# TensorE's order in a macaron block: a group's values and the output projection's halves move behind V's projection

## The reference, cut to what matters

```
x = x + 0.5 * stack(layernorm(x))       # 6 layers of attention + feed-forward
x = x + mamba(layernorm(x))             # gated convolution and a selective scan over 16 states
x = x + 0.5 * stack(layernorm(x))       # the same 6 layers again
```

```
q, k, v = split(shift(x) @ Wqkv[i])                  # 16 heads of 64
q, k = rotary(l2norm(q) * qs), rotary(l2norm(k) * ks)
sim  = q @ k' * 8, masked, windows of 32 queries against the 64 keys of this and the window before
x    = x + (softmax(sim) @ v) @ Wo[i]
h    = layernorm(shift(x)) * g + b
a, gate = split(h @ W1[i] + b1)
x    = x + (a * gelu(gate)) @ W2[i] + b2
```

## Time and profile before

| | us |
|---|---|
| median of 3 runs | 3372.07 (3358.28 to 3372.07) |
| profiled execution | 3364.97 |
| its span, first to last instruction | 3363.2 |
| PE busy | 2891.1 (86%) |
| DVE busy | 2933.3 (87%) |
| POOL busy | 2423.5 (72%) |
| ACT busy | 2059.8 (61%) |
| mean granted clock, share of full speed | 0.946 |

### The profile page before, as it was taken

How to read it: one execution, slowest core, us unless ns; L and a number is a source line. 1 busy time by engine, 2 the same in 40 slices (tenths; PEclk the granted TensorE clock), 3 DMA queues, 4 the chain that set the end, 5 groups by cost and what they waited for, 6 DMA issues and landing times. The chain is left out here.

```text
span 3363.2 us, 132089 instructions
## 1 busy us (share of the span) xinstructions
PE 2891.1 (86%) x57914; PEld 1829.9 (54%) x57914; DVE 2933.3 (87%) x4224; ACT 2059.8 (61%) x3820; POOL 2423.5 (72%) x1679
## 2 busy tenths in 40 slices
PE   5689988988999989897677788999998989998987
PEld 3455555655666655553233455555565555555553
DVE  6789989999999988986898789889899989898984
ACT  3466666666676666665663566666566666566663
POOL 3678787787787787874464678778787787787773
PEclk8899999999999999998897899999999999999998
DMA  5233333333333333320002233333343333342330
GB/s 136 65 80 77 82 91 74 84 92 71 84 92 73 89 85 72 88 65 28 10 4 59 68 81 78 75 93 77 73 101 73 86 90 71 82 94 65 88 74 15
DMA packets 114726, 250.85 MB, mean 75 GB/s; under 512 B 27244, under 2 KB 60648, under 8 KB 114152
## 3 DMA queue, kind: packets, MB, share of 16 engines
q1 hardware_dynamic: 114152, 242.40, 30.5%
HBM read 37.82 MB, written 3.15 MB: 12 GB/s over the span
## 5 line engine op out<-in xcount | busy, mean ns | idle before, releaser
L1096 ACT ACTIVATE squares<-general 128x512 f32<-128x512 f32 x768 | 453.7, 597 | 716.8 <-PE general L661 707.8
L1290 POOL TENSOR_TENSOR probs<-probs,row_sum 128x1024 f32<-128x1024 f32 x192 | 365.4, 1903 | 442.4 <-DVE row_sum L968 442.3
L1270 POOL TENSOR_TENSOR q_ring<-q_ring,partner 128x512 f32<-128x512 f32 x384 | 491.0, 1279 | 203.9 <-DMA partner<-sines 203.3
L881 DVE TENSOR_TENSOR sines<-general,layer_tables 128x512 f32<-128x512 f32 x768 | 515.8, 672 | 85.3 <-ACT squares L1096 81.8
L1270 POOL TENSOR_TENSOR k_ring<-k_ring,partner 128x512 f32<-128x512 f32 x384 | 490.9, 1278 | 0.0
L695 PE MATMUL general<-probs_t,v_buf 32*64 32x64 f32 x24576 | 339.0, 234 | 153.8 <-issue 85.1
L659 PE MATMUL general<-xs_hi,wqkv_lo 128*128 128x512 f32 x768 | 454.2, 591 | 18.5 <-DVE xs_lo L908 8.0
L695 PEld LDWEIGHTS general<-probs_t,v_buf 32*64 32x64 f32 x24576 | 304.0, 134 | 246.1 <-issue 237.5
L1284 POOL TENSOR_TENSOR probs<-probs,q_scale 128x1024 f32<-128x1024 f32 x192 | 365.4, 1903 | 15.1
L722 PE MATMUL general<-k_ring,q_ring 64*32 64x64 f32 (+1 forms) x24576 | 295.3, 223 | 92.5 <-issue 53.1
L671 PE MATMUL general<-att,wo 128*128 128x512 f32 x768 | 366.2, 621 | 4.6 <-ACT att L1166 4.2
(11 more groups left out here) (233 smaller groups left out, 6369.9 us busy)
## 6 DMA issues: line engine op xcount, KB each, us to landing
partner<-sines SPq DMA_DIRECT2D x1536, 128.0 KB, 2.3
wqkv_raw<-in_wqkv SPq DMA_DIRECT2D x80, 208.0 KB, 2.7
wo<-in_wo SPq DMA_DIRECT2D x12, 512.0 KB, 5.1
w<-in_w SPq DMA_DIRECT2D x12, 341.0 KB, 3.2
base_dram<-x SPq DMA_DIRECT2D x8, 256.0 KB, 2.4
att<-in_wqkv SPq DMA_DIRECT2D x2, 1024.0 KB, 6.7
sines<-base_dram SPq DMA_DIRECT2D x8, 256.0 KB, 3.9
w<-in_w SPq DMA_DIRECT2D x12, 128.0 KB
```

Of the source, the lines that this page charges most:

```text
L881: e.tensor_tensor(by_seq(sines[:, i % 2, which, :]), g, both(layer_tables[:, 2 * which + 1, :]), ALU.mult).then_inc(S[f"sin_{side}"], 1)
L1096: e.activation(squares[:, (2 * p + which) % 4, :], general_of(("proj", k, n, p, which))[:, :], ACT.Square).then_inc(S[f"squared_{side}"], 1)
L1270: e.tensor_tensor(y, y, partner[:, i % 2, which, :], ALU.add).then_inc(S[f"rotated_{side}"], 1)
L1290: e.tensor_tensor(y, y, spread_keys(row_sum[:, i % 2, :]), ALU.mult).then_inc(S["probs_done"], 1)
```

## The change

In `tensor_stack` V's projection now follows K's directly, then come the halves of the output projection (the second asked for before the first; they never share a substep), and the group's values last. The first half of the output projection had stood behind Q's projection and before the scores and the gates. `Banks.stack` walks in the same new order, so the banks and the waits on them change too.

```
@@ Banks.stack
-            if st.out_first:
-                n, i = st.out_first
-                self.use(("project", k, n, i), "att_added", (g + n) * 2 + i + 1)
...
+            if st.v:
+                n, p = st.v
+                self.use(("v", k, n, p), "v_kept", (g + n) * PAIRS + p + 1)
+            if st.out_last is not None:
+                self.use(("project", k, st.out_last, 1), "att_added", (g + st.out_last) * 2 + 2)
+            if st.out_first is not None:
+                self.use(("project", k, st.out_first, 0), "att_added", (g + st.out_first) * 2 + 1)
             if st.values:
                 n, group = st.values
                 for j in range(4):
                     self.use(("att", k, n, group, j), "att_kept", ((g + n) * GROUPS + group) * 4 + j + 1)
-            if st.out_last is not None:
-                self.use(("project", k, st.out_last, 1), "att_added", (g + st.out_last) * 2 + 2)
-            if st.v:
-                n, p = st.v
-                self.use(("v", k, n, p), "v_kept", (g + n) * PAIRS + p + 1)
@@ tensor_stack
                 if st.spread:
                     pe_spread(e, w, k, *st.spread)
-                if st.out_first:
-                    pe_out(e, w, k, *st.out_first)
                 if st.scores:
...
                 if st.now:
                     pe_project(e, w, k, *st.now, 1)
+                if st.v:
+                    pe_v(e, w, k, *st.v)
+                if st.out_last is not None:
+                    pe_out(e, w, k, st.out_last, 1)
+                if st.out_first is not None:
+                    pe_out(e, w, k, st.out_first, 0)
                 if st.values:
                     pe_values(e, w, k, *st.values, range(0, NWIN // 2))
-                if st.out_last is not None:
-                    pe_out(e, w, k, st.out_last, 1)
                 if st.values_rest:
                     pe_values(e, w, k, *st.values_rest, range(NWIN // 2, NWIN))
-                if st.v:
-                    pe_v(e, w, k, *st.v)
```

More of the change, by code:

```diff
@@ L34 @@
 POOL_BANKS = 7
[L37 to L45, removed]
+SCORES_LAG = 10
+SCORES_REST_LAG = 10
+SCALE_LAG = 10
+OFF_LAG = 11
+EXP_LAG = 12
+PROBS_LAG = 12
+TURN_LAG = 13
+VALUES_LAG = 14
+VALUES_REST_LAG = 14
+KEPT_LAG = 14
 V_LAG = 1
-SPREAD_LAG = SCORES_LAG
+SPREAD_LAG = 10
 PROBS = 2
@@ L108, in __init__ @@
         self.exps = self.group(t, EXP_LAG)
+        self.probs = self.group(t, PROBS_LAG)
         self.turn = self.group(t, TURN_LAG)
@@ L120, in __init__ @@
         self.spread = self.group(t, SPREAD_LAG)
-        self.out_first = next(((self.item(t, at), i) for i, at in ((0, 17),) if self.item(t, at) is not None), None)
+        self.out_first = self.item(t, 17)
+        self.first_added = self.item(t, 17)
         self.out_last = self.item(t, 21)
+        self.last_added = self.item(t, 21)
+        self.shift = self.item(t, 21)
         self.center = self.item(t, 22)
         self.var = self.item(t, 23)
+        self.var_turn = self.item(t, 23)
         self.root = self.item(t, 24)
         self.gates = self.item(t, 25)
+        self.gelus = self.item(t, 25)
         self.values_of = next(((self.item(t, at), js) for at, js in ((26, (0,)), (27, (1, 2))) if self.item(t, at) is not None), None)
+        self.hidden = next(((self.item(t, at), js) for at, js in ((26, (0,)), (27, (1, 2))) if self.item(t, at) is not None), None)
         self.ffn_out = self.item(t, 28)
+        self.ffn_added = self.item(t, 28)
+        self.ffn_shift = self.item(t, 28)
         self.load = (n // CHUNKS + 1, p) if self.now and n % CHUNKS == CHUNKS - 1 and n // CHUNKS + 1 < DEPTH else None
@@ L509, in macaron_kernel @@
             for st in PLAN:
-                for key in (("att", k, st.out_last), ("ffn", k, st.ffn_out), ("enter", k, st.enter[0] if st.enter and st.enter[1] == 2 else None)):
+                for key in (("att", k, st.shift), ("ffn", k, st.ffn_shift), ("enter", k, st.enter[0] if st.enter and st.enter[1] == 2 else None)):
                     if key[2] is not None and key[2] not in (range(ITEMS - CHUNKS, ITEMS) if key[0] == "ffn" else ()):
@@ L1008, in vector_stack @@
                     dve_scores(e, w, k, *st.scale)
-                if st.var is not None:
-                    dve_var(e, w, ("ffn", k, st.var))
-                if st.out_last is not None:
-                    dve_out(e, w, k, st.out_last, 1)
-                if st.values_of:
-                    for j in st.values_of[1]:
-                        dve_hidden(e, w, k, st.values_of[0], j)
+                if st.var_turn is not None:
+                    dve_var(e, w, ("ffn", k, st.var_turn))
+                if st.last_added is not None:
+                    dve_out(e, w, k, st.last_added, 1)
+                if st.hidden:
+                    for j in st.hidden[1]:
+                        dve_hidden(e, w, k, st.hidden[0], j)
                 if st.norms_back is not None:
@@ L1198, in scalar_stack @@
                     act_split_tokens(e, w, k, st.split)
-                if st.gates is not None:
-                    act_gelus(e, w, k, st.gates)
+                if st.gelus is not None:
+                    act_gelus(e, w, k, st.gelus)
                 if st.center is not None:
@@ L1216, in scalar_stack @@
                     act_norms_high(e, w, k, st.norms_back)
-                if st.out_last is not None:
-                    n = st.out_last
+                if st.shift is not None:
+                    n = st.shift
                     w.wait_ge(S["att_added"], (k * ITEMS + n) * 2 + 2)
@@ L1224, in scalar_stack @@
                     act_enter(e, w, k, *st.enter)
-                if st.ffn_out is not None and st.ffn_out < ITEMS - CHUNKS:
-                    n = st.ffn_out
+                if st.ffn_shift is not None and st.ffn_shift < ITEMS - CHUNKS:
+                    n = st.ffn_shift
                     w.wait_ge(S["ffn_added"], k * ITEMS + n + 1)
```

12 lines of the change are left out of this document (6 added, 6 removed).

## The result

The changed kernel took 3400.6 us (median of 4 runs, 3395.5 to 3409.3) against 3371.5 for the kernel before beside it: ratio 1.010 [1.007, 1.013]. A second series gave 1.012 [1.009, 1.015]. It is slower by 1.0 to 1.2%, 33 to 40 us; the forecast was 75. The profiled execution took 3395.49 us, span 3393.7, 30.5 above that of before.

The account below looks back on a forecast made before the run. It saw no single bound but a relay: DVE in steps 0 and 1, PE through 2 to 5, DVE through 6 and 7. 78 + 34 + 9 - 22 - 17 + 6 - 13 = +75 on 3365 gave 3440 us, range 3415 to 3470.

Parts of the forecast that it names:

- Point 1: Step 1: the second gate's bank now waits for DVE's transposition of V, so PE loses its lead; +78 us, lower bound 40.
- the 80 named: Sign of being right: PE idle before the gates, released by DVE's transposition of V, about 80 us in all.
- Point 2: Step 5: the output projection's second half starts 0.8 us later, behind V's projection, with nothing on DVE hiding it; +34 us.
- Point 3: 138 more mask matmuls on PE at 0.22 us each, only step 2's lying in PE's leg; +9 us.
- Points 4 and 5: PE's waits in steps 2 to 5 vanish, -22 us; DVE's idle time in steps 6 to 0 shrinks, -17 us.
- Point 6: Step 3's third value cut and step 5's V projection newly wait for DVE's transposition; +6 us, upper bound +42.
- Point 7: PE's unnamed stalls, read as waits for instruction blocks, shrink with V between scores and values; -13 us, bounds 0 and -138.
- a sign of being wrong: PE's leg from step 2 to DVE's addition not longer than before by the 0.8 us of the second half's delay.
- rival B: The `v_kept` waits bite, PE being tied to DVE's transposition in steps 1, 3, 5, 6 and 7; about 3490 us, chance 0.12.
- rival C: The small matmuls' stalls are the true bound and V lets instructions arrive; faster, 3315 us if all go, chance 0.05.
- A (3405): Steps 2 to 5 are not PE's leg, so PE's loss is free and only DVE's 1 us counts; chance 0.14.
- D: Nothing measurable, about 3365 us, needing three misses in one direction; chance 0.09.

Follow-up runs that it names:

- gate_twice: Changed kernel with the first gate matmul done twice, 0.8 us of added work in PE's wait for V's transposition: 1.005 of the kernel before.
- gate_bank: Changed kernel, step 0's V bank going to the output projection's first half instead of the second gate; 42 mask matmuls become ACT copies: 0.997 of the kernel before.
- first_only: Kernel before with only the output projection's first half (step 1) moved behind V's projection, V staying behind the values: 0.992 of the kernel before.
- gates_ahead: Kernel before with the output projection's first half moved only past the gates, still ahead of K's and V's projection: 0.989 of the kernel before.
- outs_only: Kernel before with both halves of the output projection moved behind V's projection, V staying behind the values: 1.000 of the kernel before.
- ties: Changed kernel with three banks exchanged: at the second gate, step 3's third value cut and step 5's V projection; only masks change hands: 0.987 of the kernel before.
- again: The changed kernel unedited, timed and profiled once more: 1.012 of the kernel before.
- v_only: Kernel before with only V's projection moved ahead of the values, both output projection halves where they were: 1.003 of the kernel before.

## Why the prediction was wrong in size and right in sign

**Point 1, the gates' bank: shown, price too high.** Where the wait ends, what is queued behind it and when step 2 and the addition come were right to 0.1 us in the item above. A grew by 2.53 us in the mean and not 1.9, since in 22 of 41 items the granted clock of A was below 0.95, at its lower level behind many of the waits; by gate_twice filling the wait is worth 15 to 22 us. By gate_bank the tie is worth 43 to 50 us net, against 78 forecast: B is 1.0 us shorter with the tie than without it, and the sum did not allow for that. PE stood 51.2 us at the gates by its own records and 88.9 by its weight loads', about the 80 named; DVE's wait came to 157.6 in 90 cases for 145 in 96.

**The step that failed** is that the first half's move was priced by its bank alone: "I give nothing for ACT having its gates earlier". Made by itself in the kernel before, the move is worth 26 us in first_only, and 38 us if the half goes only past the gates. All of the gain lies in B, the leg from step 2 to the second addition. For B points 2, 3, 4, 6 and 7 asked together for 14 us more, and it came out 27 us shorter (0.66 us in 41 items), which the prediction had itself named as a sign of being wrong. How the early gates shorten B is open: in the steady items it is not through gelus and exponentials, and the runs don't separate the mask copies from PE's waits for instructions, which fell by 31 us in first_only and by 42 in gates_ahead.

**Point 2, the second half: shown alone.** 25 us for 34, through the chain named, and 26 again from first_only to outs_only. On top of `ties` it is nothing; which work covers it there is open.

**Point 3, masks:** the counts are as said, 156 and 228. The price of the mask matmuls was not tried by itself.

**Points 4 and 5, waits given back.** PE's wait for the mask copies fell from 35.8 to 15.7 us (26.7 in the profile of again), for the 22 forecast. C shrank by 0.82 us and not 0.4. DVE's idle time in C was 0.86 us an item and not 0.5: the sum counted its waits for the squares and left out those for V's projection (13 us in the steady items), which are gone. Since first_only leaves C alone (26.04 for 26.00) and v_only shortens it (25.41), it is V's projection ahead of the values that does it, as point 5 supposed, at twice the size.

**Point 6, the other `v_kept` waits: mis-sized.** 36.1 us of PE idle time at the value cuts, and about 33 us of the total by ties against gate_bank, where I took 6 and gave 42 as the upper bound. This was rival B's mechanism; it bit, without leading to B's 3490.

**Point 7, the waits for instructions: read rightly, mis-sized.** They fell from 138 to 78 us (76 in the profile of again), by 60 and not by 13, and with them the lower clock behind them: the mean clock of B rose from 0.975 to 0.997, worth up to 27 us by my estimate (the share lost, times B, times 41 items), for which the sum had no term. The waits were not the bound, as rival C wanted: v_only removes 49 us of them and is no faster. The Trainium skill, "Runtime: NRT & Kernel Launch", section "Instruction fetch mechanics", calls fetching hidden; the trace does not agree, with 77.7 us of idle time behind packets of queue q8 still in the changed kernel.

**The rivals.** A (3405) has the nearest time, and half of its mechanism: of the 2.1 us by which the gates' tie lengthens A, 1.0 comes back in B. But the tie alone costs 43 to 50 us, over the 40 that A allows, and A has nothing for the early gates. C is refuted as above. D is outside the interval.

The experiments make a path of single steps from the kernel before to the changed one. The first half behind V's projection: -26 us (first_only). The second half too: +26 (outs_only). V's projection ahead of the values, with the gates' tie exchanged away: -10 (gate_bank against outs_only, intervals overlapping). The gates' tie: +43 to +50. Together +33 to +40. The sum had 0, 34, -37 (points 3 to 7) and 78 for them. Of the 35 to 42 us by which it was too high, 26 are the first half's move, 28 to 35 the tie and 8 the second half; 27 go the other way, because V's place brought less than the sum gave it, with point 6's waits inside.

## What to carry to other kernels

Where an engine takes banks in turn, moving a product also changes whose read every later product waits for; three exchanges of banks in the ring, with no instruction moved but some masks, turned this change from 1.2% slower into 1.3% faster. When a change moves several products, make each move by itself before pricing one at nothing: here the gates' earlier place was worth 26 to 38 us. And before a longest wait is called the cause, see whether it lies in the steady part: the 3.8 us were one case at the end of a stack. Of the orders tried, the cheapest to adopt is the first half of the output projection directly behind the gates, 0.989 of the time before.

## What was unexpected of the hardware

Waits of the same length on PE were followed by both levels of the clock: behind 25 waits of 1.61 to 1.73 us the next 3 us were granted 0.50 in 10 cases and 1.00 in 15, and behind the three of 2.67 us 0.50 each time. A redundant matmul of 0.8 us in that wait made the kernel 15 to 22 us faster. PE's unnamed gaps in the bursts of small matmuls all end 1.2 to 1.6 us behind the landing of a 16 KB packet of instructions, and in the kernel before the clock fell in or right behind such a gap in 16 of the 41 stretches B. And of two bursts of 128 small matmuls with their weight loads, the second had fewer such gaps when more of other PE work lay between them: 35.6 us for 85.1.
